# Decoder layer on one Trainium2 core: the next head's k is rotated on GpSimd instead of VectorE in the steady loops

## The chip, the cores and the metric

One core of one Trainium2 chip. The metric is the device time of one execution in microseconds. The kernel before takes 2396.72 us, the median of three runs (2395.28 to 2397.4). Engines are named as in the profile: PE (TensorE), PEld (its weight loads), DVE (VectorE), ACT (ScalarE), POOL (GpSimd), SP (SyncE, which here issues most DMA transfers).

## The reference, cut to what matters

A decoder layer over 32 sequences of 64 tokens with 512 features, in float32: a Mamba mixer, then cross-attention with rotary positions, then a routed low-rank mixture. The two parts that share the loop in question are these:

```python
# selective scan of the Mamba part, 1024 channels, 16 states
dA = jnp.exp(dt_t[..., None] * A)
dBx = dt_t[..., None] * B_t[:, None, :] * x_t[..., None]
h = dA * h + dBx
y = jnp.einsum('bdn,bn->bd', h, C_t)
...
# cross-attention, 32 query heads, 8 key heads (4 queries share a key head), D = 128
q = q * cos + _rotate_half(q) * sin
k = k * cos + _rotate_half(k) * sin
k = jnp.repeat(k, GROUPS, axis=1)
scores = jnp.einsum('bhqd,bhkd->bhqk', q, k) / jnp.sqrt(jnp.float32(D))
```

## The kernel before, in words

The 2048 tokens are taken in four blocks of 512. There are five iterations. Iteration 0 runs the Mamba part of block 0 alone. Iterations 1, 2 and 3 run the Mamba part of block i together with the attention and the mixture of block i-1. Iteration 4 runs the attention and the mixture of the last block alone. The "steady" iterations are 1 to 3: `mamba` and `attn` are both true there. All engines run programs written out by hand in one order each, with semaphores between them. Nothing is scheduled by a planner.

The inner loop of a steady iteration has 16 steps, written as 8 pairs (`jj` from 0 to 7, with `p` 0 for the even step and 1 for the odd one). A step is one state n of the scan on four chunks of channels (`c` from 0 to 3, each 128 x 1024), and at the same time one pair of query heads of the attention. Two steps, that is four query heads, share one key head. So one key head is needed for each pair of steps.

DVE, in a step of `one` in its block: multiply u by B for chunks 0 and 1 (`scan_input`, L1121), two scans (`scan`, L1130), the product with C for chunk 0 (`times_c`, L1137), `mask_scores` (L1187), `times_c` of chunk 1, `max_scores` (L1193). Then the same for chunks 2 and 3, with `invert_sum` (L1197) between the two `times_c`. At the end of the step comes `rope_q` for the query heads of the step after next (L1166, L1167, which read their first operand from PSUM), and, in even steps only, `rope_k(jj + 1)` for the next key head: L1142 (k times cos into kT), L1143 (the swapped halves kr times sin, in place), L1146 (kT minus kr, in place). All three read two operands from SBUF and are 128 x 512. They signal `krdy`.

POOL, in the same step (`sum_y`): for each chunk it waits for that chunk's `times_c` (semaphore `hcd`) and issues a DMA that adds hs[c] into xc (L706). After issues 0 and 1 it waits for the landing of chunk 2 or 3 of the step before, after issues 2 and 3 for the landing of chunk 0 or 1 of the same step (`landed`, L698, L699). Each of these posts `yad`, for which the next `scan_input` of that chunk waits. POOL computes nothing else in the steady loop.

ACT, in an odd step: copy the transposed probabilities out of PSUM (L867), `turn_k(jj + 1)` (L833, L834: the two halves of kT swapped into k2T, waits for `krdy`), the decays of chunks 2 and 3 (L888), the exponentials of the scores (L853) and more decays, `evac_o` (L876), normalisation of the probabilities (L861), and `evac_v` (L840).

PE, in a step: `turn_probs` (transposes, L1537), half of `project_o` (L1576), `scores` of the next step's heads (16 times L1526 with kT and L1528 with k2T, alternately; waits for q, `krdy` and k2T), the other half of `project_o`, `values` (L1552), `project_q` (L1496, waits until `mask_scores` has read the scores), and in odd steps `project_v` (L1510, waits for `evac_o`). The scores of step s+1 are made during step s. So the scores made in an odd step are the first ones with the new k, and those made in the even step after it use the same k.

SP, in an even step: waits for `krdy` of the current head and then loads the next head's k into k1 and kr (L514, L516).

Iterations 0 and 4 matter only as a source of rows. In iteration 0 POOL computes the scan inputs (L731, 128 x 1024, both operands in SBUF), with scans on DVE that read one operand from PSUM (L1300). In iteration 4 POOL splits weights (L666 with one input, L668 with two, 128 x 1024), while DVE runs rotations from SBUF operands. The rotation of k of iteration 4 stays on DVE, as does `rope_k(0)` ahead of each loop.

Of the kernel before, what the change touches and what calls it, by code (L numbers as in the profile page):

```python
# [21 lines left out]
ALU = mybir.AluOpType  # L22
# [57 lines left out]
def build(nc, a, out):  # L80
    ctx = ExitStack()
    with ctx:
# [560 lines left out]
        def _(eng):  # L643
# [18 lines left out]
            def one(i, mamba, attn, nxt):  # L662
# [35 lines left out]
                    eng.wait_ge(s_y[c], (i - (c == 0)) * (16 * NS) + jj * 32 + (16 * p + 16))  # L698
                    eng.sem_inc(yad.sem, 1)  # L699

                def sum_y(jj, p, first=False, last=False):

                    for c in range(NCH):
                        eng.wait_ge(hcd.sem, hcd.upto(i, NCH * p + c) + jj * (2 * NCH))
                        hold(eng)
                        G.dma_start(xc[:, 2 * c:2 * c + 2, :], hs[:, c, :].rearrange("p (d t) -> p d t", t=T),  # L706
                                    accum_op=ALU.add).then_inc(s_y[c], 16)
                        if c >= 2:
                            landed(jj, p, c - 2)
                        elif not first:  # L710
                            landed(jj - 1 if p == 0 else jj, 1 - p, c + 2)

                def begin_sum(k, at):

# [35 lines left out]
                if mamba and attn:  # L750

                    eng.wait_ge(yad.sem, yad.upto(i, -1))
                    hold(eng)
                    eng.wait_ge(y0r.sem, y0r.upto(i, NCH - 1))
                    hold(eng)
                    sum_y(0, 0, first=True)
                    sum_y(0, 1)
                    with eng.Fori(1, NS // 2 - 1) as jj:
                        sum_y(jj, 0)
                        sum_y(jj, 1)  # L760
                    sum_y(NS // 2 - 1, 0)
                    sum_y(NS // 2 - 1, 1, last=True)
                    for c in (2, 3):
                        landed(NS // 2 - 1, 1, c)
                if not mamba:
# [272 lines left out]
        def _(eng):  # L1038
# [170 lines left out]
            def one(i, mamba, attn, nxt):  # L1209
# [42 lines left out]
                def step(jj, p, tail):  # L1252

                    soft = attn and not (tail and p == 1)
                    if mamba:
                        if p == 0:
                            eng.wait_ge(ur.sem, ur.upto(i, NCH - 1))
                        eng.wait_ge(s_bc[p], i * (8 * NS) + jj * 16 + 16)
                        scan_input(i, jj, p, 0)
                        scan_input(i, jj, p, 1)  # L1260
                        scan(i, jj, p, 0)
                        scan(i, jj, p, 1)
                        times_c(i, jj, p, 0)
                    if soft:
                        mask_scores(jj, p + 1)
                    if mamba:
                        times_c(i, jj, p, 1)
                    if soft:
                        max_scores(jj, p + 1)
                    if mamba:  # L1270
                        scan_input(i, jj, p, 2)
                        scan_input(i, jj, p, 3)
                        scan(i, jj, p, 2)
                        scan(i, jj, p, 3)
                    if mamba:
                        times_c(i, jj, p, 2)
                    if soft:
                        invert_sum(jj, p + 1)
                    if mamba:
                        times_c(i, jj, p, 3)  # L1280
                    if soft and not mamba:
                        probs(jj, p + 1)
                    if not mamba:
                        o_low(jj, p)
                    if attn and not tail:
                        rope_q(jj, p + 2)
                        if p == 0:
                            rope_k(jj + 1)

                def scan_alone(jj, p, c):  # L1290
# [578 lines left out]
```

## Time and profile before

| | before |
|---|---|
| median of 3 runs | 2396.72 us (2395.28 to 2397.4) |
| the profiled execution, its own time | 2398.14 us |
| its span | 2396.3 us |
| DVE busy | 1786.4 us (75%) |
| PE busy | 2107.1 us (88%) |
| ACT busy | 1059.8 us (44%) |
| POOL busy | 588.9 us (25%), 405 instructions |
| mean granted TensorE clock | 0.942 |

The three steady loops lie at about 515 to 871, 1059 to 1416 and 1601 to 1958 us of the span. The shares in the table are averages over iterations with different limits: DVE, for instance, is at 75% over the whole span, but its share inside a steady loop is another number. A loop has to be read by its own window. In a timeline row the first number is the start in us from the span's start, the second the length in us, and a bracket at the end gives the idle time ahead of it on its engine and what ended it. A row with "x2" is two instructions of the same kind merged.

### The profile page before, as it was taken

To read this page: it belongs to the slowest core of one execution; us is meant where nothing else is said; L and a number is where in the kernel's file an instruction comes from. 1 tells how busy PE (TensorE), PEld (TensorE's weight loads), DVE (VectorE), ACT (ScalarE), POOL (GpSimd) and SP (SyncE) were. 2 spreads that over 40 slices of the span, in tenths; PEclk is the share of its full clock that TensorE was granted. 3 is DMA by queue.
4 is the path that set the end of the run, shared out by engine and by line. 5 is a ranking of instruction groups with operands and counts; after the bars stand their busy time and mean duration, and the time that the engine had idled before them with its cause. 6 is when DMAs were issued, how large, how long until landed. Compare 5 with 4: busy or idle time off the path is not lost.

```text
span 2396.3 us, 27137 instructions
## 1 busy us (share of the span) xinstructions
PE 2107.1 (88%) x8244; PEld 1194.4 (50%) x8248; DVE 1786.4 (75%) x1801; ACT 1059.8 (44%) x2613; POOL 588.9 (25%) x405
## 2 busy tenths in 40 slices
PE   6877888989999979989999979989999987799987
PEld 2332453445555534445555534445555533577763
DVE  3499994389999975289999985279999984355533
ACT  2544441465565522365665522365655521243330
POOL 0099981001111120001111110001111120566530
PEclk9888999899999989899999989889999999799888
DMA  1468893148888771238888871238888772122210
GB/s 62 166 152 198 213 213 121 54 133 187 181 177 187 166 173 53 72 123 179 176 189 179 181 172 60 72 106 172 176 196 175 171 173 82 65 90 97 88 44 18
DMA packets 110074, 328.98 MB, mean 137 GB/s; under 512 B 12945, under 2 KB 13073, under 8 KB 107569
## 3 DMA queue, kind: packets, MB, share of 16 engines
q0 software_dynamic: 35328, 127.94, 28.7%
q1 hardware_dynamic: 68912, 189.58, 26.3%
q10 hardware_dynamic: 5760, 10.49, 1.2%
q8 instruction: 45, 0.74, 0.1%
q14 instruction: 29, 0.23, 0.0%
HBM read 183.00 MB, written 14.94 MB: 83 GB/s over the span
## 4 chain that ended last, share of the span: by engine, by line
DVE 40%; PE 31%; issue 18%; DMA 5%; ACT 3%; DVEq 1%; POOL 1%; SPq 1%; POOLq 0%; ACTq 0%; PEldq 0%
DVE hs L1130 13%; PE acc L1443 5%; DVE hs L1137 5%; DVE hs L1300 5%; PE pq L1488 4%; DMA xc<-hs 3%; DVE hs L1121 3%; DVE qr L1167 2%; PE pq L1732 2%; PE pq L1496 2%; PE pq L1526 2%; PE acc L1655 2%; PE pk L1732 2%; PE acc L1565 2%; DVE sc L1187 1%
## 5 line engine op out<-in xcount | busy, mean ns | idle before, releaser
L706 POOL DMA_DIRECT2D xc<-hs x192 | 165.8, 866 | 1301.6 <-DVE hs L1137 1263.9
L1130 DVE TENSOR_TENSOR_SCAN hs<-dA,hs 128x1024 f32<-128x1024 f32 x192 | 428.9, 2276 | 0.0
L888 ACT ACTIVATE dA<-dt,aneg 128x504 f32<-128x504 f32 x384 | 253.5, 707 | 250.9 <-DVE hs L1130 250.7
L1496 PE MATMUL pq<-qT,wa 128*128 128x512 f32 x768 | 354.8, 616 | 9.2 <-DVE sc L1187 9.2
L1576 PE MATMUL acc<-wb,oT 128*128 128x512 f32 x768 | 351.7, 602 | 3.6 <-ACT oT L876 3.6
L1137 DVE TENSOR_TENSOR hs<-hs,bc 128x1024 f32<-128x1024 f32 x256 | 307.9, 1205 | 2.2
L853 ACT ACTIVATE pr<-sc,mx 128x64 f32<-128x64 f32 x512 | 170.8, 335 | 247.4 <-DVE mx L1193 247.4
L1443 PE MATMUL acc<-xnT,wa 128*128 128x512 f32 x512 | 232.2, 607 | 11.5 <-PE acc L1443 4.4
L1496 PEld LDWEIGHTS pq<-qT,wa 128*128 128x128 f32 x768 | 146.9, 197 | 183.8 <-issue 173.7
L1121 DVE TENSOR_TENSOR hs<-u,bc 128x1024 f32<-128x1024 f32 x192 | 226.3, 1219 | 8.2 <-ACT xc L976 5.9
L1526 PE MATMUL pq<-kT,qp 128*128 128x64 f32 x1024 | 190.9, 289 | 41.2 <-DVE kT L1146 16.3
L1576 PEld LDWEIGHTS acc<-wb,oT 128*128 128x128 f32 x768 | 141.1, 193 | 147.5 <-issue 143.4
L1526 PEld LDWEIGHTS pq<-kT,qp 128*128 128x128 f32 x1024 | 159.0, 205 | 78.3 <-issue 61.2
L1443 PEld LDWEIGHTS acc<-xnT,wa 128*128 128x128 f32 x512 | 96.4, 193 | 145.5 <-issue 130.5
L1528 PE MATMUL pq<-k2T,qr 128*128 128x64 f32 x768 | 154.4, 284 | 0.0
L1528 PEld LDWEIGHTS pq<-k2T,qr 128*128 128x128 f32 x768 | 122.4, 201 | 0.0
L731 POOL TENSOR_TENSOR qp<-u,bc 128x1024 f32<-128x1024 f32 x32 | 92.9, 2904 | 107.8 <-ACT xc L976 107.6
L1187 DVE COPY_PREDICATED sc<-mask,pq 128x512 f32<-128x512 int32 x64 | 46.7, 729 | 88.3 <-PE pq L1528 45.6
L731 POOL TENSOR_TENSOR qr<-u,bc 128x1024 f32<-128x1024 f32 x32 | 100.2, 3130 | 7.6 <-DVE hs L1300 7.6
L1079 DVE SCALAR_TENSOR_TENSOR xc<-acc,cw,xc 128x504 f32<-128x504 f32 (+2 forms) x96 | 69.9, 734 | 42.1 <-ACT xc L811 39.6
L1510 PEld LDWEIGHTS pk<-wv,ctxT 128*128 128x128 f32 x768 | 87.5, 192 | 27.4 <-issue 26.4
L1510 PE MATMUL pk<-wv,ctxT 128*128 128x128 f32 x768 | 92.0, 278 | 7.7 <-ACT oT L876 7.7
(200 smaller groups left out, 3312.7 us busy)
## 6 DMA issues: line engine op xcount, KB each, us to landing
xc<-hs POOLq DMA_DIRECT2D x240, 512.0 KB, 6.9
bc<-bc_rows SPq DMA_DIRECT2D x64, 512.0 KB, 7.5
wa<-in_wq SPq DMA_DIRECT2D x64, 512.0 KB, 10.2
wb<-in_wo SPq DMA_DIRECT2D x64, 512.0 KB, 5.8
wa<-in_wx SPq DMA_DIRECT2D x16, 512.0 KB, 4.2
wa<-in_wz SPq DMA_DIRECT2D x16, 512.0 KB, 4.9
wb<-in_ow SPq DMA_DIRECT2D x16, 512.0 KB, 7.2
k<-k_rows SPq DMA_DIRECT2D x32, 256.0 KB, 11.1
```

Source lines behind the costliest of these rows:

```text
L731: G.tensor_tensor(inputs[c % 2].rearrange("p (d t) -> p d t", t=T), u[:, 2 * c:2 * c + 2, :], bc[:, p, 0:1, :].to_broadcast([P, 2, T]), AL ...
L853: ins = S.activation(pr[:, b, :], sc[:, b, :], ACT.Exp, bias=mx[:, b:b + 1], accum_out=sm[:, b:b + 1])
L888: ins = S.activation(to[:, :, 1:SEQ], dt[:, s, :].rearrange("p (b t) -> p b t", t=SEQ)[:, :, 1:SEQ], ACT.Exp, scale=aneg[:, s, bass.ds(jj ...
L1121: V.tensor_tensor(hs[:, c, :].rearrange("p (d t) -> p d t", t=T), u[:, 2 * c:2 * c + 2, :], bc[:, p, 0:1, :].to_broadcast([P, 2, T]), ALU. ...
L1130: V.tensor_tensor_scan(out=hs[:, c, :], data0=dA[:, c % 2, :], data1=hs[:, c, :], initial=0.0, op0=ALU.mult, op1=ALU.add).then_inc(scd.sem, 1)
L1137: V.tensor_tensor(h3, h3, bc[:, p, 1:2, :].to_broadcast([P, 2, T]), ALU.mult).then_inc(hcd.sem, 1)
L1443: ins = M.matmul(banks(s % 4), wa4((s // 2) % 2)[:, k, (s % 2) * P:(s % 2 + 1) * P], xnT[:, k, :], start=(k == 0), stop=(k == KE - 1))
L1496: ins = M.matmul(pq[:, h, :], wa4(p)[:, k, h * P:(h + 1) * P], qT[:, k, :], start=(k == 0), stop=(k == KE - 1))
L1510: ins = M.matmul(pk[:, 1, t * D:(t + 1) * D], ctxT[:, k, t * P:(t + 1) * P], wv[:, k, :], start=(k == 0), stop=(k == KE - 1))
L1526: ins = M.matmul(pq[:, 0, seq], qp[:, b, :], kT[:, seq], start=True, stop=not mamba)
L1528: ins = M.matmul(pq[:, 0, seq], q2[:, b, :], k2T[:, seq], start=False, stop=True)
L1576: ins = M.matmul(acc[:, t, :], oT[:, h, t * P:(t + 1) * P], wb2(o % 2)[:, h, :], start=False, stop=(stop and h == 1))
```

## The change

In steady iterations `rope_k(jj + 1)` is no longer called by DVE. A function `turn_next_k(jj)` on POOL issues the same three instructions with the same waits (the k transfers landed, the scores that read the old kT done), and the same `krdy` signal. It stands in `sum_y` after the loop over the four chunks of an even step, that is behind the fourth DMA issue and behind the wait for chunk 1's landing, and ahead of the first issue of the odd step. It is left out in the last pair. DVE goes from `rope_q` of the even step straight to the odd step.

```diff
+                def turn_next_k(jj):
+
+                    g, b = jj + 1, i - 1
+                    eng.wait_ge(s_k1, b * (16 * KVH) + g * 16 + 16)
+                    eng.wait_ge(s_kr, b * (32 * KVH) + g * 32 + 32)
+
+                    eng.wait_ge(sd.sem, sd.upto(b, -1) + g * 2)
+                    hold(eng)
+                    G.tensor_tensor(kT[:, :], k1[:, :], cosT[:, :], ALU.mult).then_inc(kt1.sem, 1)
+                    G.tensor_tensor(kr[:, :], kr[:, :], sinT[:, :], ALU.mult).then_inc(kt2.sem, 1)
+                    eng.wait_ge(kt1.sem, kt1.upto(b, 0) + g)
+                    eng.wait_ge(kt2.sem, kt2.upto(b, 0) + g)
+                    G.tensor_tensor(kT[:, :], kT[:, :], kr[:, :], ALU.subtract).then_inc(krdy.sem, 1)
+
-                def sum_y(jj, p, first=False, last=False):
+                def sum_y(jj, p, first=False, last_pair=False):
...
                             landed(jj - 1 if p == 0 else jj, 1 - p, c + 2)
+                    if p == 0 and not last_pair:
+                        turn_next_k(jj)
...
-                    sum_y(NS // 2 - 1, 0)
-                    sum_y(NS // 2 - 1, 1, last=True)
+                    sum_y(NS // 2 - 1, 0, last_pair=True)
+                    sum_y(NS // 2 - 1, 1)
...
                         rope_q(jj, p + 2)
-                        if p == 0:
+                        if p == 0 and not mamba:
                             rope_k(jj + 1)
```

POOL's program in the loop over the middle pairs, from the third issue of an even step to the first issue of the odd step, before:

```order
L706 DMA xc<-hs 128x1024 [waits state_times_c]
L698 ISA
L704 REGISTER_ALU [waits y_summed0]
L706 DMA xc<-hs 128x1024 [waits state_times_c]
L698 ISA
L704 REGISTER_ALU [waits y_summed1]
L706 DMA xc<-hs 128x1024 [waits state_times_c]
```

and now (`y_summed1` is the landing of chunk 1, `scores_done` the scores that read the old kT):

```order
L720 DMA xc<-hs 128x1024 [waits state_times_c]
L698 ISA
L704 ISA [waits y_summed1]
L705 ISA [waits k_loaded]
L707 ISA [waits k_halves_loaded]
L709 TENSOR_TENSOR kT<-k1,cosT 128x512 [waits scores_done]
L710 TENSOR_TENSOR kr<-kr,sinT 128x512
L711 ISA
L713 TENSOR_TENSOR kT<-kT,kr 128x512 [waits k_times_sin,k_times_cos]
L718 REGISTER_ALU
L720 DMA xc<-hs 128x1024 [waits state_times_c]
```

The three instructions stand between the fourth issue and the next step's first issue. The issues themselves keep their order.

DVE's program at the end of an even step and the start of the odd one, before:

```order
L1166 TENSOR_TENSOR qp<-pq,cosT 128x2x8x64 [waits scores_done,q_done]
L1167 TENSOR_TENSOR qr<-pq,sinT 128x2x8x64
L1173 ISA
L1174 ISA [waits k_loaded]
L1176 ISA [waits k_halves_loaded]
L1142 TENSOR_TENSOR kT<-k,cosT 128x512 [waits scores_done]
L1143 TENSOR_TENSOR kr<-kr,sinT 128x512
L1144 REGISTER_ALU
L1146 TENSOR_TENSOR kT<-kT,kr 128x512 [waits k_times_sin,k_times_cos]
L1121 TENSOR_TENSOR hs<-u,bc 128x1024 [waits y_added,bc_loaded1]
```

and now, where L1182 and L1183 are `rope_q` and L1137 is `scan_input`, L1146 the scan:

```order
L1182 TENSOR_TENSOR qp<-pq,cosT 128x2x8x64 [waits scores_done,q_done]
L1183 TENSOR_TENSOR qr<-pq,sinT 128x2x8x64
L1137 TENSOR_TENSOR hs<-u,bc 128x1024 [waits y_added,bc_loaded1]
L1137 TENSOR_TENSOR hs<-u,bc 128x1024 [waits y_added]
L1144 REGISTER_ALU
L1146 SCALAR_TENSOR_TENSOR hs<-dA,hs 128x1024 [waits decay_ready,scan_input_ready]
```

The three instructions are gone from DVE; nothing else of its order has changed.

## Rows read from the trace of the kernel before

**Rows 1.** Busy time by engine in one stretch of a steady loop.

```profile
core 0: us, PE busy (x) PEld busy (x) DVE busy (x) ACT busy (x) POOL busy (x), PEclk, DMA share, GB/s
626.00:671.00 45.00, 42.67 (x202) 25.39 (x201) 44.90 (x39) 26.28 (x75) 6.88 (x8) 1.00 0.85 182
```

**Rows 2.** Timeline of DVE, one pair of steps: start us, us, engine, line.

```profile
657.22 0.73 DVE L1187 COPY_PREDICATED sc<-mask,pq 128x512 f32<-128x512 int32 x1
...
667.44 1.17 DVE L1137 TENSOR_TENSOR hs<-hs,bc 128x1024 f32<-128x1024 f32 x1
...
670.80 0.68 DVE L1142 TENSOR_TENSOR kT<-k,cosT 128x512 f32<-128x512 f32 x1
...
672.18 0.69 DVE L1146 TENSOR_TENSOR kT<-kT,kr 128x512 f32<-128x512 f32 x1
672.79 2.35 DVE L1121 TENSOR_TENSOR hs<-u,bc 128x1024 f32<-128x1024 f32 x2
675.06 4.47 DVE L1130 TENSOR_TENSOR_SCAN hs<-dA,hs 128x1024 f32<-128x1024 f32 x2
...
701.91 0.72 DVE L1187 COPY_PREDICATED sc<-mask,pq 128x512 f32<-128x512 int32 x1
```

**Rows 3.** Timeline of ACT in the odd step, behind the rotated k.

```profile
672.91 0.63 ACT L833 ACTIVATE k2T<-kT 64x512 f32<-64x512 f32 x1 [1.90 <-DVE kT L1146]
...
677.49 0.72 ACT L888 ACTIVATE dA<-dt,aneg 128x504 f32<-128x504 f32 x1 [3.31 <-DVE hs L1130]
```

**Rows 4.** Timeline of PE through the same pair of steps.

```profile
652.95 0.33 PE L1526 MATMUL pq<-kT,qp 128*128 128x64 f32 x2
...
667.68 0.59 PE L1496 MATMUL pq<-qT,wa 128*128 128x512 f32 x1
...
674.32 0.41 PE L1526 MATMUL pq<-kT,qp 128*128 128x64 f32 x2 [0.51 <-ACT k2T L834]
...
690.09 3.83 PE L1510 MATMUL pk<-wv,ctxT 128*128 128x128 f32 x32 [0.37 <-ACT oT L876]
...
697.63 0.33 PE L1526 MATMUL pq<-kT,qp 128*128 128x64 f32 x2
...
700.93 0.39 PE L1528 MATMUL pq<-k2T,qr 128*128 128x64 f32 x2
```

**Rows 5.** Timeline at a mask that waited for its scores: PE, then DVE.

```profile
472.70 0.63 PE L1528 MATMUL pq<-k2T,qr 128*128 128x64 f32 x2
...
473.51 0.72 DVE L1187 COPY_PREDICATED sc<-mask,pq 128x512 f32<-128x512 int32 x1 [15.75 <-PE pq L1528]
```

**Rows 6.** POOL: fourth issue of an even step, and landing times of all its issues.

```profile
669.19 0.86 POOL L706 DMA_DIRECT2D xc<-hs  x1 [0.34 <-issue]
...
DMA to landing us min/median/max: 4.5/7.2/15.1
```

**Rows 7.** Iteration 4, timelines: a two-input POOL instruction, DVE's two-input one beside it.

```profile
2068.61 2.34 POOL L668 TENSOR_TENSOR wq_lo<-wa,wq_hi 128x1024 fp32r<-128x1024 f32 x1
...
2068.81 3.21 DVE L1143 TENSOR_TENSOR qr<-qr,sinT 128x1024 f32<-128x1024 f32 x1
2072.13 1.23 DVE L1146 TENSOR_TENSOR qp<-qp,qr 128x1024 f32<-128x1024 f32 x1
```

**Rows 8.** Iteration 4, two orders of arrival: DVE and POOL timelines.

```profile
2031.58 0.69 DVE L1142 TENSOR_TENSOR kT<-k,cosT 128x512 f32<-128x512 f32 x1
2032.18 1.53 DVE L1143 TENSOR_TENSOR kr<-kr,sinT 128x512 f32<-128x512 f32 x1
...
2031.90 3.00 POOL L666 TENSOR_SCALAR wq_hi<-wa 128x1024 fp32r<-128x1024 f32 x1 [41.89 <-DMA wa<-in_wq]
...
2157.52 0.68 DVE L1143 TENSOR_TENSOR kr<-kr,sinT 128x512 f32<-128x512 f32 x1
...
2157.54 3.29 POOL L666 TENSOR_SCALAR wo_hi<-wb 128x1024 fp32r<-128x1024 f32 x1 [4.16 <-PE acc L1565]
...
2098.14 2.77 POOL L666 TENSOR_SCALAR wq_hi<-wa 128x1024 fp32r<-128x1024 f32 x1 [0.68 <-POOL wo_lo L668]
```

## The prediction

> **What bounds the kernel now.** I read the busy time of each engine in a stretch of a steady loop first. DVE is busy 44.90 us of 45.00 there and PE 42.67 us, at a granted clock of 1.00 [rows 1]. That is where the page's 75% for DVE misleads: in the loop DVE is full, and PE is nearly so. Then the timeline of DVE. `mask_scores` of an even step starts at 657.22 and of the next even step at 701.91 [rows 2]. So a pair of steps takes 44.69 us. It is DVE's own work, without a gap. Last the timelines of ACT and PE, for what waits for the rotated k. ACT starts to copy kT into k2T at 672.91, 0.04 after DVE's last instruction of k, which ends at 672.87 [rows 2, 3]. PE's scores start at 674.32 and had waited 0.51 for that copy [rows 4]. So k is already the last thing to arrive at PE in every odd step.
>
> **A second chain is almost as long as DVE's.** Followed from mask to mask through k it has these pieces. DVE from the mask (657.22) to the end of the even step's last product with C (667.44 + 1.17 = 668.61): 11.39 us [rows 2]. From there to k ready at 672.87: 4.26. From k ready to PE's first score, through ACT: 674.32 - 672.87 = 1.45. PE from these scores to the next ones, 674.32 to 697.63, is 23.31 with a wait of 0.37 for ACT at `project_v` in it, so 22.94 of work in a fixed order [rows 4]. The scores themselves: 700.93 + 0.39 - 697.63 = 3.69. From their end to a mask that waited for them: 473.51 - (472.70 + 0.63) = 0.18 [rows 5]. Sum: 43.91 us. DVE's 44.69 exceeds it by 0.78 us. **This 0.78 is all that k may come later before the pair gets longer.** The same slack read directly: 0.37 at `project_v`, and 701.91 - 701.32 - 0.18 = 0.41 at the mask.
>
> **The change, part by part.** The three instructions leave DVE in 7 pairs of each of three loops, 21 times. From the first of them to the next `scan_input` is 672.79 - 670.80 = 1.99 us [rows 2], so DVE alone would gain 21 x 1.99 = 41.8 us. SP's loads of the next k wait for `krdy`, but in the next even step, some 20 us later, so nothing there moves. POOL's next issue, the odd step's first, comes with the product of chunk 0, over 10 us after the fourth one, so POOL is free again in time. The landings that DVE waits for next are posted ahead of the new instructions. The new wait for chunk 1's landing is the old one, only with k queued behind it: landings take 7.2 us in the median and 15.1 at most [rows 6], and I cost it at nothing. If it came late, k would be late by as much. ACT has `turn_k` ahead of the odd step's decays, which begin at 677.49 after 3.31 idle [rows 3]. A k that is 2.7 us later still fits there.
>
> **When k is ready on POOL.** The fourth issue starts at 669.19 and takes 0.86 [rows 6]. So the first multiply starts at about 670.05. No row of the steady loop shows such an instruction on POOL. The nearest is L668: two SBUF inputs, 128 x 1024, 2.34 us [rows 7]. Half of that is 1.17. I take 1.2 for 128 x 512, since the fixed part does not halve (DVE's own takes 0.68). Three of them, with 0.1 for the wait ahead of the third, would be 3.7 us if DVE left them alone.
>
> **It does not.** At 2068.81 DVE starts an instruction with two SBUF inputs, 0.20 after POOL's two-input L668. It takes 3.21 us; the next of the same size takes 1.23 [rows 7]. So it stood until about 2070.80, 0.15 before POOL's ended. In the other direction POOL's L666 takes 3.29 us beside DVE's L1143, and 2.77 alone [rows 8]. Whoever is late waits. Behind `rope_q`, which reads one operand from PSUM, DVE's next instructions are `scan_input`, twice, and scans. All of these read two operands from SBUF. Now DVE reaches the first one at 670.80, in the middle of POOL's first multiply. (Or 0.3 later, once the mask waits for its scores: `project_q` ends 667.68 + 0.59 - 652.95 = 15.32 after the first score [rows 4], `rope_q` can start 0.18 after that, and that mask starts 3.87 after the first score; so 11.6 from mask to `rope_q`, against 11.3 now.) How they take turns: at 2031.90 POOL comes while L1142 runs on DVE, and DVE's next instruction, which starts at 2032.18, is the one held (1.53 for 0.68) [rows 8]. So a waiting POOL gets in at the end of the DVE instruction that is running. That gives, on the clock of rows 2: POOL 1 from 670.05 to 671.25, with its reads done at 671.10. `scan_input` 1 from then to about 672.35. POOL 2 from 672.20 to 673.40. `scan_input` 2 from 673.25 to 674.47. POOL 3, there since 673.50, from 674.32 to 675.52. Then the scan. **k is ready at 675.52, that is 2.65 us later than before.** The Trainium skill (SBUF — State Buffer, "Who interferes with whom") says that a DVE instruction with two SBUF inputs contends with a GpSimd one that reads SBUF, and that the loser waits for the whole instruction. The rows agree for POOL's two-input instruction, all but its last 0.15; with the whole 1.2 held at each turn k would be 0.27 later and the sum below 6 us higher.
>
> A price that only a page has: the Trainium skill (GPSIMD Engine Reference, "Elementwise — side-by-side cycle accounting") gives 4497 ns for a two-input add of 2048 elements. A quarter is 1.12 us, and the sum would be some 3 to 5 us lower by it.
>
> **The sum.** The chain through k becomes 43.91 + 2.65 = 46.56 us. DVE alone would have 44.69 - 1.99 + some 2.3 of waiting for POOL = 45.0. So the chain bounds the pair, and it is 1.87 us longer than 44.69. 21 x 1.87 = 39.3 us. The profiled execution took 2398.14 us of its own time, which makes 2437; it stands 1.4 above the median of the runs, 2396.72. Against the median the forecast is **2436 us**, 1.6% slower. DVE will show idle time again, at the even step's mask, and the freed 1.99 us will lie in it. PE stays at its work without waiting in the odd step.
>
> **Rivals.**
> (a) DVE and POOL meet, but POOL's second multiply is in ahead of `scan_input`. DVE, if 0.3 late, comes at 671.1, and POOL's second at about 671.2: they arrive within 0.1 us of each other. Then k takes 4.5 us instead of 5.47, and the pair gains 0.88 over 44.69: 18.5 us, 2415.
> (b) POOL's three are not disturbed (3.7 us). k is ready at 673.75, 0.88 late, 0.10 beyond the slack: 2 us, so 2399. For it: the rows of contention are from another iteration and of twice the size. The gain on DVE would still be lost, since k was the last to arrive before. This is the case of no change.
> (c) Faster. The mechanism: DVE is the only bound, and PE and ACT take a later k without passing it on. Place: the 0.78 us of slack. The deciding point: k ready before 673.4, which makes POOL's three 3.35 us or less, or a slack of over 2.7 us. Its full price is the 41.8 us above: 2355. For it speaks DVE at 44.90 of 45.00; against it PE's 0.51 wait for k2T and the 42.67 of 45.00, which leave no room. Even at 1.17 per instruction and undisturbed, k is 0.79 late, which is just the slack.
> (d) POOL is held longer. At 2157.54 it comes just after L1143 has started on DVE, close behind the instruction before, and waits it out [rows 8]. If both `scan_input` pass ahead of POOL 2, and then a scan (4.47 for two) ahead of POOL 3, k is ready at 677.7, 4.83 late: 4.05 a pair, 85 us, 2482.
>
> **How the numbers follow.** Forecast as worked out, with the multiply between 1.1 and 1.35 us and the start on POOL up to 0.3 later: 56%, 2426 to 2450. (a) 14%, 2408 to 2425. Between the forecast and (d), with parts of it: 16%, half of it up to 2455. (b) 8%. (c) 6%. The range that leaves out (b), (c) and the upper half of (d) is 2408 to 2455. About 0.2% (5 us) is what a measurement of this kernel can tell from no change. Faster by more than that: (c), 0.06. Within it: (b), 0.08. Slower: 0.86.
>
> **What would show it.** In the profile of the changed kernel: POOL's three instructions start some 0.9 us after the fourth issue; the second and third take up to 2.3 us from start to end, since they include the wait for DVE; the two `scan_input` and the first scan of an odd step are longer than 2.35 and 2.24 us by some 2 us together; ACT's `turn_k` begins near 7 us after the last product with C, where it was 4.3; DVE idles 1 to 2 us at the even step's mask, released by PE's scores; PE shows no wait at `project_v` any more. A pair takes 46.5 us. The forecast is wrong if DVE's `scan_input` keeps its 1.13 us spacing, or if the masks of even steps still follow their DVE predecessor without a gap. Then (b) or (c) holds.

## The result, and the profile after

The changed kernel takes 2507.87 us, the median of four runs (2506.48 to 2509.05). The kernel before took 2396.69 beside it (2395.28 to 2397.4). The medians differ by 111 us. The ratio of the runs is 1.0449 with a 95% interval of 1.0428 to 1.047, which is 103 to 113 us slower. The forecast was 2436 with a range up to 2455. So the sign was right and the size was not. The profiled execution took 2506.48 us of its own time.

The page of the kernel after: busy times, the granted clock in 40 slices, and the chain of work that ended last, by engine.

```profile
PE 2192.0 (88%) x8244; PEld 1262.5 (50%) x8248; DVE 1809.2 (72%) x1738; ACT 1059.6 (42%) x2613; POOL 686.4 (27%) x468
...
PEclk9888999889989999898998899989899889799888
...
PE 56%; DVE 18%; issue 12%; POOL 5%; DMA 4%; ACT 3%; SPq 1%; DVEq 0%; POOLq 0%; ACTq 0%; PEldq 0%
```

The same three of the page before:

```profile
PE 2107.1 (88%) x8244; PEld 1194.4 (50%) x8248; DVE 1786.4 (75%) x1801; ACT 1059.8 (44%) x2613; POOL 588.9 (25%) x405
...
PEclk9888999899999989899999989889999999799888
...
DVE 40%; PE 31%; issue 18%; DMA 5%; ACT 3%; DVEq 1%; POOL 1%; SPq 1%; POOLq 0%; ACTq 0%; PEldq 0%
```

DVE has 63 instructions fewer (3 x 21), and yet it is busy 22.8 us longer: it is held. The chain went over from DVE to PE. And PE is busy 84.9 us longer with the same 8244 matmuls. The mean granted clock, 0.942 before, is 0.909 now.

The busy times of one stretch of the first steady loop, after and then before (columns as in [rows 1]), show it without the other iterations:

```profile
560.00:800.00 240.00, 221.98 (x966) 138.36 (x965) 217.72 (x162) 123.07 (x347) 56.30 (x54) 0.91 0.74 163
```

```profile
560.00:800.00 240.00, 228.28 (x1078) 135.84 (x1076) 239.48 (x198) 139.31 (x396) 36.19 (x42) 1.00 0.85 185
```

The granted clock was 1.00 in the loop and is 0.91. DVE falls from 239.48 to 217.72 of 240. A pair of steps, 44.69 us before, now takes 49.9 in the mean. In the timeline of DVE the first and the last mask of an even step in this loop are seven pairs apart:

```profile
524.35 0.72 DVE L1203 COPY_PREDICATED sc<-mask,pq 128x512 f32<-128x512 int32 x1
...
873.90 0.73 DVE L1203 COPY_PREDICATED sc<-mask,pq 128x512 f32<-128x512 int32 x1 [1.05 <-PE pq L1544]
```

That is 349.55 us for seven. (Single pairs lie between 48.9 and 51.0.) The difference of 5.2 us, 21 times, is 109 of the 111 us. So nearly all of it lies in the pairs that the change touches.

**When k comes.** Timelines of POOL, ACT and DVE at the end of an even step, after:

```profile
686.80 0.86 POOL L720 DMA_DIRECT2D xc<-hs  x1 [0.34 <-issue]
687.52 1.44 POOL L709 TENSOR_TENSOR kT<-k,cosT 128x512 f32<-128x512 f32 x1
688.76 1.42 POOL L710 TENSOR_TENSOR kr<-kr,sinT 128x512 f32<-128x512 f32 x1
690.33 2.07 POOL L713 TENSOR_TENSOR kT<-kT,kr 128x512 f32<-128x512 f32 x1
```

```profile
692.43 0.63 ACT L849 ACTIVATE k2T<-kT 64x512 f32<-64x512 f32 x1 [3.81 <-POOL kT L713]
```

```profile
663.66 1.22 DVE L1182 TENSOR_TENSOR qp<-pq,cosT 128x1024 f32<-128x1024 f32 x1 [2.51 <-PE pq L1512]
...
674.84 0.73 DVE L1203 COPY_PREDICATED sc<-mask,pq 128x512 f32<-128x512 int32 x1 [1.06 <-PE pq L1544]
...
685.06 1.17 DVE L1153 TENSOR_TENSOR hs<-hs,bc 128x1024 f32<-128x1024 f32 x1
...
688.53 4.95 DVE L1137 TENSOR_TENSOR hs<-u,bc 128x1024 f32<-128x1024 f32 x2
693.40 4.46 DVE L1146 TENSOR_TENSOR_SCAN hs<-dA,hs 128x1024 f32<-128x1024 f32 x2
...
699.82 0.73 DVE L1203 COPY_PREDICATED sc<-mask,pq 128x512 f32<-128x512 int32 x1 [0.84 <-PE pq L1544]
```

DVE's last product with C ends at 685.06 + 1.17 = 686.23, and k is ready at 690.33 + 2.07 = 692.40: 6.17 us, where it was 4.26 [rows 2]. So k is 1.91 us late. POOL starts its first multiply 0.72 behind the start of the fourth issue, and the second 1.24 later. DVE's two `scan_input` take 4.95 together, 2.60 more than in [rows 2]. DVE arrives at 688.53 and POOL's second at 688.76. POOL's second is no longer than its first (1.42 and 1.44), so it did not wait; its third, 2.07, did. If each instruction needs about 1.2 us alone, the times fit only one order: POOL, POOL, DVE, POOL, DVE. POOL went in twice running although DVE was already waiting. DVE now idles at the masks of both steps (674.84 is the even step's, 699.82 the odd one's) and at the odd step's `rope_q`, for PE each time.

**What PE does with it.** Timeline of PE in the same place, after:

```profile
687.34 0.66 PE L1553 MATMUL pk<-ident,pr 128*128 128x128 f32 x4 [1.11 <-ACT pr L877]
...
693.85 0.41 PE L1542 MATMUL pq<-kT,qp 128*128 128x64 f32 x2 [2.42 <-ACT k2T L850]
694.09 0.39 PE L1544 MATMUL pq<-k2T,qr 128*128 128x64 f32 x2
...
694.98 0.39 PE L1544 MATMUL pq<-k2T,qr 128*128 128x64 f32 x2
695.21 0.59 PE L1542 MATMUL pq<-kT,qp 128*128 128x64 f32 x2
695.58 0.64 PE L1544 MATMUL pq<-k2T,qr 128*128 128x64 f32 x2
...
699.00 0.63 PE L1544 MATMUL pq<-k2T,qr 128*128 128x64 f32 x2
...
719.83 0.33 PE L1542 MATMUL pq<-kT,qp 128*128 128x64 f32 x2
```

PE waited 0.51 for k2T before [rows 4] and waits 2.42 now, 1.91 more. The first six groups of scores go at their old pace, 0.23 us from one to the next. Then the same matmuls, back to back, with nobody to wait for, take 0.43 each. From the scores that waited for k to the next step's first ones PE needs 719.83 - 693.85 = 25.98 us here, and 27.6 to 27.7 in four of the loop's seven pairs, 26.9 in the mean. Before, this was the 22.94 of work in the prediction. Short stretches of the same place, with the granted clock behind the busy times:

```profile
687.00:694.00 7.00, 4.24 (x14) 2.01 (x14) 7.00 (x5) 2.13 (x5) 5.25 (x4) 1.00 0.92 149
694.00:697.00 3.00, 3.00 (x21) 3.00 (x22) 3.00 (x2) 1.18 (x2) 0.00 (x0) 0.71 1.03 284
697.00:700.00 3.00, 3.00 (x14) 2.87 (x14) 2.16 (x3) 1.47 (x3) 0.44 (x1) 0.50 0.65 152
```

PE was busy 4.24 of 7.00 us at the full clock of 2.4 GHz. Then, with PE busy again, the granted clock went to 0.50, its other level, 1.2 GHz. At 0.91 in the mean a pair of 49.9 us has some 9 us at that level ((1 - 0.91) / 0.5 x 49.9), and work that PE would do in 4.5 us takes 9 there (both are estimates from the mean clock). It happens in each pair. Before, PE idled at the same two places, 1.5 and 0.5 us at most in the window from 560 to 800, and the clock stayed at 1.00.

**The account.** With the lateness as measured, the prediction's chain gives 43.91 + 1.91 = 45.82 us a pair: 21 x 1.13 = 24 us. The rest, 49.9 - 45.8 = 4.1 us a pair, 86 us, is what the prediction did not have. PE's path from the odd step's scores to the next ones, 4.0 longer (26.9 for 22.94), makes up nearly all of that rest. The first theory, called A in the expectations, puts these 86 us on PE's clock, which falls because PE idles longer than before (1.11 and 2.42 us within 8). Its rival, B, puts the loss on the contention of POOL and DVE in SBUF: the held DVE. The trace alone doesn't decide between them. DVE shows both the 2.6 us of being held and the idling.

### The profile page after: what moved, and what is told of

The parts are those of the page before. It is cut to its first block, busy times and chain, and to the rows that moved or that the text cites. A ratio compares the mean times of both kernels' runs of the same rounds, so it can differ in the third digit from the quotient of the medians.

```text
span 2504.5 us, 27155 instructions
## 1 busy us (share of the span) xinstructions
PE 2192.0 (88%) x8244; PEld 1262.5 (50%) x8248; DVE 1809.2 (72%) x1738; ACT 1059.6 (42%) x2613; POOL 686.4 (27%) x468
## 4 chain that ended last, share of the span: by engine, by line
PE 56%; DVE 18%; issue 12%; POOL 5%; DMA 4%; ACT 3%; SPq 1%; DVEq 0%; POOLq 0%; ACTq 0%; PEldq 0%
PE acc L1592 9%; PE pq L1512 8%; PE pq L1542 6%; PE acc L1459 5%; PE pq L1544 4%; DVE hs L1146 4%; PE pq L1504 4%; DVE hs L1316 4%; PE pk L1526 3%; DMA xc<-hs 2%; PE pk L1568 2%; PE pq L1748 2%; PE acc L1671 2%; POOL kT L713 2%; PE acc L1581 2%
## 5 line engine op out<-in xcount | busy, mean ns | idle before, releaser
L1146 DVE TENSOR_TENSOR_SCAN hs<-dA,hs 128x1024 f32<-128x1024 f32 x192 | 428.5, 2272 | 0.0
L1592 PE MATMUL acc<-wb,oT 128*128 128x512 f32 x768 | 390.0, 657 | 3.6 <-ACT oT L892 3.6
L1542 PE MATMUL pq<-kT,qp 128*128 128x64 f32 x1024 | 220.8, 324 | 82.0 <-ACT k2T L850 51.6
L1137 DVE TENSOR_TENSOR hs<-u,bc 128x1024 f32<-128x1024 f32 x192 | 281.3, 1505 | 6.6 <-ACT xc L992 5.9
L1542 PEld LDWEIGHTS pq<-kT,qp 128*128 128x128 f32 x1024 | 187.7, 238 | 119.2 <-issue 102.0
L1592 PEld LDWEIGHTS acc<-wb,oT 128*128 128x128 f32 x768 | 156.8, 215 | 171.1 <-issue 167.0
L1544 PE MATMUL pq<-k2T,qr 128*128 128x64 f32 x768 | 186.8, 334 | 0.0
L1544 PEld LDWEIGHTS pq<-k2T,qr 128*128 128x128 f32 x768 | 153.7, 248 | 0.0
L1182 DVE TENSOR_TENSOR qp<-pq,cosT 128x1024 f32<-128x1024 f32 x48 | 58.8, 1224 | 65.1 <-PE pq L1512 64.5
L869 ACT ACTIVATION_READ_ACCUMULATOR pr<-sc,mx 128x1 f32 x512 | 95.8, 187 | 0.0
```

The costliest lines, as they stand in the source:

```text
L869: ins = S.activation(pr[:, b, :], sc[:, b, :], ACT.Exp, bias=mx[:, b:b + 1], accum_out=sm[:, b:b + 1])
L1137: V.tensor_tensor(hs[:, c, :].rearrange("p (d t) -> p d t", t=T), u[:, 2 * c:2 * c + 2, :], bc[:, p, 0:1, :].to_broadcast([P, 2, T]), ALU. ...
L1146: V.tensor_tensor_scan(out=hs[:, c, :], data0=dA[:, c % 2, :], data1=hs[:, c, :], initial=0.0, op0=ALU.mult, op1=ALU.add).then_inc(scd.sem, 1)
L1542: ins = M.matmul(pq[:, 0, seq], qp[:, b, :], kT[:, seq], start=True, stop=not mamba)
L1544: ins = M.matmul(pq[:, 0, seq], q2[:, b, :], k2T[:, seq], start=False, stop=True)
L1592: ins = M.matmul(acc[:, t, :], oT[:, h, t * P:(t + 1) * P], wb2(o % 2)[:, h, :], start=False, stop=(stop and h == 1))
```

## The experiments

Each kernel was timed beside the kernel before on the same chip, and each ratio is to that. The copies and products that experiments add write into buffers that nobody reads; the matmuls that they add put zeros onto `acc`. None leaves work of the kernel out.

**1. The changed kernel with PE kept busy.** Ten matmuls of zeros, which add zero to `acc`, stand in PE's odd steps ahead of the scores that wait for k, in the time in which PE idled.

```diff
                         project_o(jj, p - 1, 0, False)
+                    if mamba and p == 1 and not tail:
+                        for n in range(10):
+                            M.matmul(acc[:, n % TT, :], zeros[:, 0:P], zeros[:, :], start=False, stop=False)
```

> The changed kernel, plus ten bf16 matmuls of zeros into acc (start=False, so they add nothing) on PE, ahead of the scores of each odd step, where PE now idles for 2.42 us behind k2T. Theory A (k comes 1.91 us later, PE idles, the granted clock falls to its lower level for 7 to 10 us per pair, and PE at 1.2 GHz makes the pair long): the clock stays at 1.00, what is left is the chain through k, 44.69 + 1.91 - 0.78 = 45.8 us per pair, so 2397 + 21 x 1.13 = about 2421 us. Theory B (DVE and POOL hold each other up at the SBUF port, and this is the loss): nothing changes for them, 2505 to 2510 us.

Measured: 2425.69 us (2418.11 to 2426.68), ratio 1.0103 [1.0072, 1.0134], 25.8 us over its own kernel before (2399.91). PE does more work and the kernel is some 82 us faster than the changed one. Theory A had said 2421, B 2505 or more. Busy times in the loop, and what is left of the wait for k2T:

```profile
560.00:800.00 240.00, 232.75 (x1117) 139.78 (x1116) 239.19 (x180) 137.94 (x388) 59.09 (x57) 1.00 0.81 176
```

```profile
684.26 0.41 PE L1542 MATMUL pq<-kT,qp 128*128 128x64 f32 x2 [0.26 <-ACT k2T L850]
```

The granted clock is 1.00 again in this stretch, and a pair takes 45.63. (In the third loop it fell in one pair, behind a PE wait of 2.46 for the probabilities, and that pair took 48.2.) DVE is busy 239.19 of 240, with the two `scan_input` still at 4.95. So with the clock held DVE, held by POOL, is nearly full again: 44.69 - 1.99 + 2.60 = 45.3 by itself. The 0.3 between 45.3 and 45.63 is short gaps of DVE ahead of the even step's mask (0.2) and of `rope_q` (0.1), which both wait for PE. Chain and DVE are about equally long here, so this run alone doesn't say which of the two makes the 25 us.

**2. k late without POOL.** The kernel before, with three idle ACT copies between ACT's wait for k and its copies into k2T. POOL and DVE do exactly what they did.

```diff
-                def turn_k(g):
+                def turn_k(g, extra=()):
                     eng.wait_ge(krdy.sem, krdy.upto(blk, 0) + g)
+                    for x in extra:
+                        S.activation(x[:, :], cosT[0:SSM, :], ACT.Copy)
...
-                        turn_k(jj + 1)
+                        turn_k(jj + 1, (ssq, rms, ssmT,))
```

> The kernel before plus three such idle copies: k2T is ready 1.91 us later, as much as in the changed kernel, but POOL has nothing to do with it and DVE is not held up at any port. Theory A: PE idles 2.4 us ahead of the odd scores, the granted clock falls in most pairs, a pair takes 49 to 50 us: 2490 to 2510 us. Theory B: only the chain, 2397 + 24 = 2421, or less.

Measured: 2503.77 us (2503.19 to 2505.31), ratio 1.0439 [1.0419, 1.046]. This is nearly all of the change's loss, and no instruction of POOL was added. The three copies delay k2T by 1.68 us, not by the 1.91 that the expectation says: ACT starts the first at 691.89 and the copy into k2T at 693.57.

```profile
560.00:800.00 240.00, 222.88 (x969) 137.37 (x968) 216.86 (x179) 134.59 (x368) 33.23 (x39) 0.92 0.74 163
```

```profile
694.98 0.41 PE L1528 MATMUL pq<-kT,qp 128*128 128x64 f32 x2 [2.32 <-ACT k2T L836]
```

The wait of PE (2.32), the clock (0.92), DVE's busy time (216.86) and the pair (49.8) are close to those of the changed kernel (2.42, 0.91, 217.72, 49.9). So lateness at PE is enough to make the loss, with DVE undisturbed. B falls as the cause of the 86 us.

**3. The same with the ten matmuls of zeros.** It takes the clock out of experiment 2 and leaves the chain alone, undisturbed by POOL. Its edit is those of 1 and 2 together.

> e3_late3 (k2T 1.91 us late through idle copies on ACT, k rotated on DVE) plus the ten zero matmuls of e1_warm on PE. It separates the chain from the port: no POOL instruction is in it, and the clock should hold. Theory A': what is left is the chain alone, 43.91 + 1.91 = 45.82 us per pair, 2397 + 24 = 2421 us. If it is well below e1_warm's 2424, part of e1_warm was the port; if the same, the chain alone would have made it too.

Measured: 2416.01 us (2414.71 to 2418.97), ratio 1.0057 [1.0035, 1.0079].

```profile
560.00:800.00 240.00, 233.67 (x1120) 139.79 (x1120) 235.56 (x196) 144.32 (x399) 36.24 (x42) 1.00 0.84 181
```

The clock is 1.00, a pair takes 45.52, and DVE is no longer full. It waits at the mask for PE. In experiment 2 PE's wait for k2T was 2.32 where it had been 0.51, so k comes 1.81 late there, and the chain of the prediction fed with this says 43.91 + 1.81 = 45.72: 0.2 too much. (The expectation's 45.82 has 1.91.) PE's work from the odd step's scores to the next ones takes 22.68 here, where the prediction had 22.94. The clock is 2503.77 - 2416.01 = 88 us of experiment 2. The chain is 14 us by the ratio and 17 by the pairs (21 x 0.83).

**4. POOL's part by itself.** The kernel before, whose DVE rotates k in time, and three idle POOL products with two SBUF inputs behind that.

```diff
+                    if p == 0 and not last:
+                        eng.wait_ge(krdy.sem, krdy.upto(i - 1, 1) + jj)
+                        for n, x in enumerate((ssq, rms, ssmT)):
+                            G.tensor_tensor(x[:, :], cosT[0:SSM, :], sinT[0:SSM, :], ALU.mult).then_inc(s_dummy, 1)
+                        eng.wait_ge(s_dummy, (i - 1) * 21 + jj * 3 + 3)
```

> The kernel before, k rotated on DVE and on time, plus three two-input products on POOL (64 x 512, into buffers that are free there; nothing reads them) behind the fourth issue of each even step but the last, started when k is ready. They meet scan_input, scan_input and the scan of the odd step. It measures the port by itself. DVE is held three times for what POOL reads, about 1.1 to 1.25 us each: a pair takes 44.69 + 3.5 = 48.2 us, 2397 + 21 x 3.5 = 2470 us, with k never late. If PE's longer idle time lets the clock fall here too, the clock shows it, and it costs less, since PE then has 3.5 us of room. Theory A alone (the port costs nothing): 2397.

Measured: 2466.54 us (2466.53 to 2468.04), ratio 1.0265 [1.0242, 1.0289]. The busy times of the loop, and timelines of DVE and of POOL:

```profile
560.00:800.00 240.00, 217.61 (x1008) 128.65 (x1007) 239.48 (x188) 130.46 (x373) 72.38 (x55) 0.98 0.78 169
```

```profile
682.77 3.42 DVE L1127 TENSOR_TENSOR hs<-u,bc 128x1024 f32<-128x1024 f32 x2
686.12 6.56 DVE L1136 TENSOR_TENSOR_SCAN hs<-dA,hs 128x1024 f32<-128x1024 f32 x2
```

```profile
682.94 2.17 POOL L716 TENSOR_TENSOR ssq<-cosT,sinT 64x512 f32<-64x512 f32 x1 [2.91 <-DVE kT L1152]
685.08 2.24 POOL L716 TENSOR_TENSOR rms<-cosT,sinT 64x512 f32<-64x512 f32 x1
687.28 3.24 POOL L716 TENSOR_TENSOR ssmT<-cosT,sinT 64x512 f32<-64x512 f32 x1
```

`scan_input` is held 3.42 - 2.35 = 1.07 us and the scans 6.56 - 4.47 = 2.09: 3.16 together. The pair became 47.87 - 44.69 = 3.18 longer. DVE is full here (239.48 of 240), so each microsecond of being held is one of time. Contention does have its price, and here it is paid in full. In the changed kernel it lay beside PE's longer path. One POOL product of 64 x 512 costs a full DVE about 1.05 us here, and the three of 128 x 512 in experiment 7 hold DVE for 3.1, as much. DVE's own k multiply takes it 0.68. So to move one of them under two-input work of DVE is a loss even without a chain. The clock fell here too, in the first four pairs of the first loop (0.98 in the stretch) and in most of the third (0.96), and almost never cost anything: those pairs took 47.86 like the others, but for one of 49.14. While DVE is the longer path, a slower PE is hidden behind it.

**5. k a little late.** As experiment 2, but with one idle copy.

```diff
-                        turn_k(jj + 1)
+                        turn_k(jj + 1, (ssq,))
```

> The kernel before, k rotated on DVE, plus one idle 64x512 copy on ACT between the wait for k and the copies into k2T in each odd step: k2T is ready 0.64 us later, less than the 0.78 us of slack. Theory A: 2397 us, no change (within 5 us), the clock stays at 1.00 in the loops. A rival C (every delay of k passes on): 21 x 0.64 = 13 us, 2410.

Measured: 2439.59 us (2438.61 to 2447.01), ratio 1.0179 [1.0149, 1.0209]. No theory had this. The lateness (0.64) is within the slack of 0.78, and the first pairs take 44.69 and 44.68, as before. Then the clock falls, and from there each pair takes 47.8. (In the second loop it fell from the first of these pairs on, in the third only after three.) Two stretches of the first loop:

```profile
560.00:630.00 70.00, 65.98 (x303) 38.48 (x302) 69.79 (x59) 41.34 (x115) 10.61 (x13) 1.00 0.83 185
```

```profile
640.00:800.00 160.00, 152.84 (x679) 91.39 (x678) 149.23 (x123) 89.64 (x255) 22.43 (x27) 0.93 0.79 170
```

PE waits 1.16 for k2T in the pairs at full clock and 1.29 in the others. So the same lateness has two costs. There are two ways of running, and the loop goes from one to the other.

**6. The same three instructions one issue earlier**, behind the third issue of the even step.

```diff
-                    if p == 0 and not last_pair:
-                        turn_next_k(jj)
+                        if c == 2 and p == 0 and not last_pair:
+                            turn_next_k(jj)
```

> All three on POOL, behind the third issue instead of the fourth. The multiplies meet only rope_q, the subtraction meets scan_input. k is ready at about 673.5, 0.6 later than before, inside the slack; DVE waits for POOL about 0.4 + 1.1 us and has 1.99 less: 44.2 us per pair if the clock holds, 2387 us. e2_late1 shows that a lateness of 0.64 is enough to let the clock fall once something starts it; then 47 to 48 us per pair, 2430 to 2450. I expect the second.

Measured: 2416.58, 2443.76 and 2467.52 us in three runs; the ratio, of the two shorter ones, is 1.0114 [1.0043, 1.0184]. Inside the execution of 2443.76 us the loops differ. These are the same stretch of its first, second and third loop:

```profile
560.00:800.00 240.00, 227.63 (x1007) 137.90 (x1006) 224.27 (x172) 129.77 (x370) 57.37 (x56) 0.93 0.78 172
1110.00:1350.00 240.00, 228.27 (x1097) 138.24 (x1097) 239.18 (x186) 140.84 (x405) 60.98 (x59) 1.00 0.83 183
1650.00:1890.00 240.00, 228.32 (x1022) 137.72 (x1022) 225.88 (x175) 132.46 (x374) 57.42 (x56) 0.94 0.77 173
```

The second loop keeps the full clock and takes 44.44 us a pair, less than before. The other two take 47.77. PE waits 1.23 for k2T in either kind. So the same program with the same wait runs both ways. That a run's time depends on how many pairs fall would explain the spread: the mean granted clocks of the three runs, 0.932, 0.919 and 0.911, go down as the times go up. But only this one execution has a trace.

**7. Two issues earlier**, behind the second issue of the even step. k is in time, and POOL's three meet DVE's scans.

```diff
-                    if p == 0 and not last_pair:
-                        turn_next_k(jj)
+                        if c == 1 and p == 0 and not last_pair:
+                            turn_next_k(jj)
```

> The changed kernel, but the three instructions stand behind the second issue of the even step, some 9 us earlier, beside two-input instructions and scans of DVE. k is ready long before PE wants it. Theory A: no wait for k2T at PE; DVE loses the port time of three POOL instructions (3 x 1.25 = 3.7 us) and has 1.99 us less to do, so a pair takes 46.4 us and the kernel 2397 + 36 = 2433, if the clock holds (PE then idles about 4 us per pair, in other places). Theory B: the port is the loss, and there is at least as much meeting as before: 2500 us or more.

Measured: 2454.26 us (2450.88 to 2455.76), ratio 1.0229 [1.0206, 1.0252]. That lies between the theories, nearer to A's figure than to B's, and for a reason that neither had. POOL, DVE and PE:

```profile
668.68 2.13 POOL L709 TENSOR_TENSOR kT<-k,cosT 128x512 f32<-128x512 f32 x1 [0.43 <-DMA kr<-k_rows]
670.77 3.25 POOL L710 TENSOR_TENSOR kr<-kr,sinT 128x512 f32<-128x512 f32 x1
674.17 3.07 POOL L713 TENSOR_TENSOR kT<-kT,kr 128x512 f32<-128x512 f32 x1
```

```profile
669.60 6.57 DVE L1146 TENSOR_TENSOR_SCAN hs<-dA,hs 128x1024 f32<-128x1024 f32 x2
676.09 2.22 DVE L1153 TENSOR_TENSOR hs<-hs,bc 128x1024 f32<-128x1024 f32 x1
```

```profile
680.53 1.08 PE L1553 MATMUL pk<-ident,pr 128*128 128x128 f32 x4 [4.16 <-ACT pr L877]
```

The scans are held 2.1 us and the product with C 1.0. DVE hands the sums to ACT that much later, ACT the normalised probabilities, and PE idles 4.16 at `turn_probs`. So even with k early PE has its long wait, from another engine, and the clock is 0.96. A pair takes 47.7, where A had 46.4 with the clock held. The trace reads as if the contention reaches the clock by way of DVE; no run of this kernel with the clock held tests it.

**8. One instruction on POOL.** Only k1 times cos runs on POOL, behind the third issue, beside `rope_q`, which reads PSUM. DVE does the other two where it did all three.

```diff
-                    eng.wait_ge(s_kr, b * (32 * KVH) + g * 32 + 32)
-
...
-                    G.tensor_tensor(kr[:, :], kr[:, :], sinT[:, :], ALU.mult).then_inc(kt2.sem, 1)
-                    eng.wait_ge(kt1.sem, kt1.upto(b, 0) + g)
-                    eng.wait_ge(kt2.sem, kt2.upto(b, 0) + g)
-                    G.tensor_tensor(kT[:, :], kT[:, :], kr[:, :], ALU.subtract).then_inc(krdy.sem, 1)
...
+                def finish_k(g):
+                    eng.wait_ge(s_kr, blk * (32 * KVH) + g * 32 + 32)
+                    V.tensor_tensor(kr[:, :], kr[:, :], sinT[:, :], ALU.mult).then_inc(kt2.sem, 1)
+                    eng.wait_ge(kt1.sem, kt1.upto(blk, 0) + g)
+                    eng.wait_ge(kt2.sem, kt2.upto(blk, 0) + g)
+                    V.tensor_tensor(kT[:, :], kT[:, :], kr[:, :], ALU.subtract).then_inc(krdy.sem, 1)
```

> Only the first multiply (k1 times cos into kT) on POOL, and behind the third issue of the even step, where DVE runs rope_q, which reads one operand from SBUF. The second multiply and the subtraction stay on DVE behind rope_q. By the port reading: POOL's 1.42 us lies from 668.7 to 670.1, nothing of DVE waits, DVE has 0.60 us less per pair, k is 0.6 earlier, the clock holds: 44.09 us per pair, 2397 - 21 x 0.60 = 2384 us. A rival (any POOL compute there costs DVE as much as it takes away): 2397 to 2405.

Measured: 2389.37 us (2381.87 to 2397.1), ratio 0.9955 [0.9937, 0.9973], that is 0.3 to 0.6% faster. A pair takes 44.09, that is 0.60 less than 44.69, about what one DVE instruction of k took (0.68). The clock stays at 1.00.

**9. Two instructions on POOL.** Both multiplies run behind the third issue, and DVE subtracts behind `rope_q`. The edit is that of 8 with the second multiply left on POOL, and only the subtraction on DVE.

> Both multiplies on POOL behind the third issue, the subtraction on DVE behind rope_q. POOL: 668.7 to 671.4, beside rope_q (668.5 to 670.9). DVE waits 0.5 us for it and then subtracts: its next scan_input starts at 672.1 instead of 672.8, k is 0.7 earlier, the fourth issue is 2.4 us later, which its landing time allows. 44.0 us per pair, 2397 - 21 x 0.7 = 2382 us. Rival: POOL is held by the product with C of chunk 3 (two SBUF inputs, to 668.6), so both end 0.3 or more later: 2390 to 2400.

Measured: 2389.89 us (2383.97 to 2393.32), ratio 0.9951 [0.9934, 0.9968]. A pair takes 43.98. The second one brings next to nothing more, because DVE waits for it:

```profile
673.20 0.69 DVE L1196 TENSOR_TENSOR kT<-kT,kr 128x512 f32<-128x512 f32 x1 [0.60 <-POOL kr L710]
```

**10. The same, with the subtraction behind the first `scan_input` of the odd step**, which fills that wait.

```diff
                         scan_input(i, jj, p, 0)
+                        if attn and p == 1 and not tail:
+                            finish_k(jj + 1)
                         scan_input(i, jj, p, 1)
```

> c2_two, but DVE subtracts behind the first scan_input of the odd step, so that it does not stand 0.60 us waiting for POOL ahead of it. scan_input 1 reaches the port at 670.8 on the clock of the kernel before and is held to about 671.3, the subtraction ends at about 673.0: k 0.15 later than before, DVE has 0.85 us less per pair. With the clock held: 43.85 us per pair, 2397 - 18 = 2379. If 0.15 is enough to let it fall: 2430 or more.

Measured: 2383.45 us (2382.25 to 2387.04), ratio 0.992 [0.9896, 0.9945]. It beats the kernel before by 0.5 to 1.0%, and the changed one by 5%. The intervals of experiments 8, 9 and 10 overlap, so which of the three is best isn't shown. Timelines of POOL and DVE, and the loop:

```profile
668.60 1.41 POOL L709 TENSOR_TENSOR kT<-k,cosT 128x512 f32<-128x512 f32 x1
669.84 1.40 POOL L710 TENSOR_TENSOR kr<-kr,sinT 128x512 f32<-128x512 f32 x1
```

```profile
670.75 1.57 DVE L1134 TENSOR_TENSOR hs<-u,bc 128x1024 f32<-128x1024 f32 x1
672.25 0.68 DVE L1196 TENSOR_TENSOR kT<-kT,kr 128x512 f32<-128x512 f32 x1
```

```profile
560.00:800.00 240.00, 229.94 (x1092) 138.09 (x1090) 239.36 (x191) 141.57 (x402) 48.79 (x53) 1.00 0.86 186
```

Only the end of POOL's second multiply meets DVE's `scan_input` (1.57 for some 1.2). k is ready at 672.25 + 0.68 = 672.93, which is 4.46 after the last product with C (667.29 + 1.18), 0.20 later than before. DVE is full, the clock is 1.00 in this stretch, a pair takes 43.9. In the last pair of the second loop the clock fell all the same, and that pair took 47.26.

## Why the prediction was wrong in size and right in sign

- **What bounds the kernel now.** DVE full at 44.69, a chain through k of 43.91, a slack of 0.78: this held. Experiment 3 gave the chain 45.52 where the same pieces said 45.72. But "all that k may come later before the pair gets longer" was wrong. In experiment 5 k came late within the slack, and after two pairs of the first loop each one took 3.1 us more.
- **The three leave DVE, 41.8 us by itself.** They left, and the time went into being held: 2.60 us a pair, more than the 1.99 freed (predicted 2.3).
- **When k is ready.** Predicted 2.65 late, measured 1.91. The step that failed is "a waiting POOL gets in at the end of the DVE instruction that is running" taken as taking turns. Here it was DVE that waited, and POOL's second multiply, 0.23 us behind DVE's arrival, still went in first. That is the order of rival (a), which had 14%. Behind it k takes 4.88 us from the first multiply, where (a) said 4.5. The estimate of 1.2 us per multiply was good (1.24). The start came 0.14 earlier than the end of the issue.
- **The sum.** The term for the chain alone was 39 us, and with the measured lateness it is 24 (experiments 1 and 3: 25 and 14 to 17). **The step that failed is "PE from these scores to the next ones ... 22.94 of work in a fixed order".** That work was priced at the full clock. There [rows 1] have 1.00 and a PE busy 42.67 of 45.00. I read the 1.00 as a property of the chip, where it is a result of how PE is fed. The sum holds a longer wait of PE for k (0.51 and the lateness), but nothing that follows from it, and the text beside it says that "PE stays at its work without waiting in the odd step": it waits 2.42. With waits of 1.11 and 2.42 us within 8 the clock falls, and the 22.94 become 26.0 to 27.7, some 27. That is 86 of the 111 us, shown by experiments 1 and 3 (they give 82 and 88 back) and by 2, which makes the loss without POOL. The chain's 24 us, without the clock, would have given 2421, inside the range.
- **The rivals.** (b) and (c) are out. (d), with 2482, was nearest in time, and wrong: its place was a k 4.83 late. None of the rivals had the clock. The Trainium skill (TensorE: Matmul & The Clock Gate, "HAM oscillation — how this bites in real kernels") tells of a matmul loop in which PE waits in each iteration and starts the next at the lower clock, every time. The traces here agree that a loop can do this, with waits of 1.1 and 2.4 us ahead of each fall. It would have been the rule to weigh against the 0.51 of [rows 4].
- **What would show it.** Of the signs named, these came: `turn_k` 6.2 us after the last product with C (said: near 7), DVE idle 1.06 at the even step's mask, no wait at `project_v`, a third POOL instruction of 2.07, the start of the first 0.72 after the issue (said: 0.9). These didn't: a pair of 46.5 (49.9), and idling at the even step's mask alone (the odd step's mask, 0.5 to 2.0, and `rope_q`, up to 2.6, have it too). The scans kept their 4.46 for two; all 2.60 us of being held lie in the two `scan_input`.

## What to carry to other kernels

Where a forecast prices PE's work at a granted clock of 1.00, price a new wait of PE twice: once as time, and once as work after it at half the clock, in each iteration. Here a slack of 0.78 us worked out at the full clock didn't cover the second price. Not every wait costs it (in experiment 10 one pair of 21 did), and it was hidden where DVE was the longer path (experiment 4). Moving instructions from VectorE to GpSimd paid here where they ran beside VectorE work that reads PSUM; where VectorE waited for the end of the second one (experiment 9), that one brought next to nothing. Beside two-input work from SBUF one cost the full VectorE about 1.05 us, where the instruction itself had cost 0.68.

## What the runs showed of the hardware beyond that

- **Two ways of running.** In experiments 5 and 6 the same loop ran at 44.4 to 44.7 us a pair with the clock at 1.00, or at 47.8 with it falling in each pair, with 1.16 to 1.29 us of PE waiting for k2T in either. Once fallen, it fell in every later pair of those loops. In experiment 4, with DVE full, it fell in the first four pairs of the first loop and then stopped, and in experiment 1 it fell in one pair alone. In the changed kernel and experiment 2 (mostly 2.3 to 2.4 us) the clock fell in every pair, in the kernel before (0.5) in none between a loop's first pair and its last. In experiment 10 it held through a wait of 1.41 in the first loop and fell in the second behind one of 0.72. So the length of the wait for k2T does not settle it, and what starts it is open. That the slower pass itself moves the waits so that the clock falls again would fit, and wasn't tried.
- **A held instruction is not always held by turns.** POOL went in twice running ahead of a waiting DVE in the changed kernel. In experiment 4 the three POOL products took 2.17, 2.24 and 3.24 us, which fits DVE going in between them (how long such a product takes alone no run shows). The start on POOL behind a DMA issue was 0.72 us after that issue's start, within its 0.86.
- **Scans contend too.** DVE's scans, with both inputs in SBUF, took 6.56 and 6.57 us for two in experiments 4 and 7, and 4.47 beside an idle POOL. The Trainium skill (SBUF — State Buffer, "Who interferes with whom") says this of a VectorE instruction with two SBUF inputs, and the scans agree. `rope_q`, with one operand in PSUM, kept its 1.2 us beside POOL's multiplies (experiments 9 and 10), as the same section has it.
